# Mixing stage: the sums and differences of each chunk stored by SyncE instead of GpSimd

## The chip, the cores and the metric

The kernel runs on one core of one Trainium2 chip. The metric is device time in microseconds (us), the median over the runs.

## What is computed

The reference works on an input of 4 batches x 32 channels x 128 x 128 pixels in float32. A first layer (an attention over spectral convolutions) comes first and takes about two thirds of the time. The change lies in the second layer, which is a full spectral convolution:

```
x = x + irfft2( sum_i rfft2(norm(x))[b, i, :, :] * W[i, o, :, :] )      # W complex, 32 x 32 x 128 x 65
```

For each frequency the 32 input channels are mixed into 32 output channels by a complex matrix of its own. The weights are two float32 tensors, real and imaginary, of 34 MB each, and every one of their rows is read once.

## The kernel before

The second layer is a block of its own (the last `with ExitStack()` in the code, `p8`), and its mixing stage goes through 32 chunks (`NCHK`). A chunk `c_` holds two rows of frequencies and the two mirrored ones, and each of its buffers exists twice; `u = c_ % 2` picks one.

- **Weights.** `load_weights(eng, p, c_)` issues two transfers, real and imaginary, of 520 KB each (32 x 32 runs of 520 bytes) into the halves of `wsl[u]`. SyncE issues the pair for `p = 0`, ScalarE the pair for `p = 1`. Both wait until the chunk two before has been mixed (`s_ms`), because that frees the buffer. The last chunk takes two rows that don't lie side by side, and its pair of SyncE comes in runs of 260 bytes.
- **Columns.** GpSimd copies the columns of the spectrum of the chunk two ahead into `cols` (L1978, L1979).
- **Spectrum.** TensorE's `spectrum` (L2022) makes the spectrum rows of a chunk. ScalarE's and VectorE's `rows` copy them into `xsl[u]`, tile `pa`.
- **Mixing.** TensorE's `mix` (L2035) waits for all four weight transfers of the chunk (`s_w[u]`), for the rows, and for the PSUM tile `po[u]`. It makes 130 small matmuls and then raises `s_ms`. The trace holds two records for each of them.
- **Pairing.** ScalarE copies the lower half (`neg`, L2109). VectorE's `pairs(c_)` makes sums and differences into `osl[:, u]` (L2176 to L2187) and raises `s_oc`.
- **Storing.** GpSimd's `store(c_)` waits for the pairs and issues two transfers of 128 KB from `osl` to the DRAM tensor `os_` (L1988), in runs of 512 bytes. `pairs(c_ + 2)` waits until they have landed (`s_os[u]`).

After the 32 chunks SyncE waits for all stores and loads `os_` back in pieces (L1949). TensorE, ScalarE and VectorE turn these back into pixels, and SyncE stores the output (L1955, four transfers of 128 KB in runs of 512 bytes for each piece). The matrices for that, `eo` and `cf`, are loaded by SyncE behind the last weight load (L1941).

Each engine takes its instructions in order, and so does each engine's queue of transfers. SyncE's transfers are on queue q1 of the profile, ScalarE's on q10, GpSimd's on q0, where software makes the descriptors. All of them use the same 16 DMA engines.

Of the kernel before, what the change touches and what calls it, by code (L numbers as in the profile page):

```python
# [14 lines left out]
NB, NT, NHD = 4, 32, 32  # L15
# [22 lines left out]
SL = 2  # L38
NCHK = HH // 2 // SL
SM = SL * KWF  # L40
NP = HH // 2
# [146 lines left out]
def wait(eng, sem, value):  # L188

    if not (isinstance(value, int) and value <= 0):  # L190
        eng.wait_ge(sem, value)


def per_batch(eng, body):

    body(0)
    with eng.Fori(1, NB) as b:
        body(b)
# [8 lines left out]
def build(nc, a, c, out):  # L207
# [5 lines left out]
    def dram(name, shape):  # L213
        return nc.dram_tensor(name, shape, F32, kind="Internal").ap()
# [10 lines left out]
    os_ = dram("os_", (HH, 4, NT, NB * 32))  # L225
# [6 lines left out]
    def sems(name, n):  # L232

        return [sem(f"{name}_{i}") for i in range(n)]

    def sem(name):
        assert name not in names
        names.add(name)
        h = nc.alloc_semaphore(name=name)
        if name not in POOL_TRANSFERS:  # L240
            held.append(h)
        return h


    with top:
# [44 lines left out]
        with ExitStack() as p1:  # L290
            def sb(name, shape):
                return p1.enter_context(nc.sbuf_tensor(name, shape, F32))
# [66 lines left out]
            @block.sync  # L359
            def _(sp):  # L360
                for i in range(4):
                    n = HH * WW // 4
                    sp.dma_start(xa[:, i * n:(i + 1) * n], xf[:, i * n:(i + 1) * n]).then_inc(s_x[i // 2], 16)

                def load(b):
                    for u in range(GPB):

                        wait(sp, s_f1, GPB * b + u + 1 - GPB)
                        sp.dma_start(xd[:, u, :].rearrange("h (g w) -> h g w", g=GI),
                                     x[bass.ds((b * GPB + u) * GI, GI)].rearrange("g h w -> h g w")).then_inc(s_xd[u], 16)  # L370
                per_batch(sp, load)
                sp.wait_ge(s_mtr, 1)
                sp.dma_start(mpl.rearrange("m (z k h) -> k (m z) h", z=2, k=KW), mtr.rearrange("w m r h -> w (m r) h")).then_inc(s_wv, 16)

                def spectra_back(b):
                    for q in s_xs:
                        sp.wait_ge(q, 16 * (GPB // 2) * (b + 1))
                    sp.dma_start(room[32 * b:32 * b + 32, 0:2 * M2], xs[32 * b:32 * b + 32].rearrange("i m k -> i (m k)")).then_inc(s_xt, 16)
                for b in range(1, NB - 1):
                    spectra_back(b)  # L380
                sp.wait_ge(s_wt, 1)
                spectra_back(0)
                spectra_back(NB - 1)
                sp.wait_ge(s_wv, 16)
# [982 lines left out]
        def lagged(b, u, k, body, *args):  # L1367

            if k > u:
                if not (isinstance(b, int) and b == 0):  # L1370
                    body(b - 1, u - k + GPB, *args)
            else:
                body(b, u - k, *args)
# [497 lines left out]
        with ExitStack() as p8:  # L1871
# [20 lines left out]
            osl = sb("osl", [128, 2, 2, SL, NB, 32])  # L1892
# [14 lines left out]
            s_ms, s_nc, s_oc, s_pt8 = sem("chunk_mixed"), sem("lower_mixed_copied"), sem("mixed_chunk_paired"), sem("p8_pair_steps")  # L1907
            s_os = sems("mixed_chunk_stored", 2)
# [6 lines left out]
            def load_weights(eng, p, c_):  # L1915

                u = c_ % 2
                if p == 1:
                    row0, step = HH // 2 - SL * (c_ + 1), 1
                elif c_ < NCHK - 1:  # L1920
                    row0, step = HH // 2 + 1 + SL * c_, 1
                else:
                    row0, step = HH // 2, HH // 2 - 1
                for r, w in enumerate((a["L1_conv_weight_real"], a["L1_conv_weight_imag"])):
                    q = slice(64 * p + 32 * r, 64 * p + 32 * r + 32)
                    if step == 1:
                        src, dst = bass.AP(w.tensor, row0 * KWF, [[NT * HH * KWF, NT], [HH * KWF, NT], [1, SM]]), wsl[u][q]
                    else:
                        src = bass.AP(w.tensor, row0 * KWF, [[NT * HH * KWF, NT], [HH * KWF, NT], [step * KWF, SL], [1, KWF]])
                        dst = wsl[u][q].rearrange("p o (q w) -> p o q w", q=SL)  # L1930
                    eng.dma_start(dst, src).then_inc(s_w[u], 16)  # L1931

            @block.sync
            def _(sp):
                for t, n in ((gmean, "gmean"), (wide, "wide")):
                    sp.dma_start(t[:, :], c[n]).then_inc(s_ld, 16)
                for c_ in range(NCHK):
                    wait(sp, s_ms, c_ - 1)
                    load_weights(sp, 0, c_)
                for t, n in ((eo, "eo"), (cf, "cf")):  # L1940
                    sp.dma_start(t[:, :], c[n]).then_inc(s_eo, 16)  # L1941

                for q in s_os:
                    sp.wait_ge(q, 32 * NCHK // 2)

                def load(b, u):
                    g = GPB * b + u
                    wait(sp, s_h, g + 1 - GPB)
                    sp.dma_start(od[:, u], os_[:, :, bass.ds(2 * g, 2), :].rearrange("s f o m -> s f (o m)")).then_inc(s_od[u], 16)  # L1949

                def store(b, u):
                    g = GPB * b + u
                    sp.wait_ge(s_fin, g + 1)
                    for i in range(NB):
                        sp.dma_start(xob[:, i, bass.ds(2 * g, 2), :], yb[:, i, bass.ds(2 * g, 2), :]).then_inc(s_st, 16)  # L1955

                def body(b):
                    for u in range(GPB):
                        lagged(b, u, 0, load)
                        lagged(b, u, 3, store)  # L1960
                per_batch(sp, body)
                for k in (3, 2, 1):
                    store(NB - 1, GPB - k)
                sp.wait_ge(s_st, 16 * NB * NGRP)

            @block.gpsimd
            def _(pool):
                y1v = y1[:, :, :].rearrange("w i (s k) -> w k s i", s=2)

                def columns(c_):  # L1970

                    u = c_ % 2
                    wait(pool, s_sp, c_ - 1)
                    if c_ < NCHK:
                        near = y1v[:, SL * c_ + 1:SL * c_ + 3]
                        if c_ == NCHK - 1:
                            pool.wait_ge(s_b0, 1)
                        nc.gpsimd.tensor_copy(cols[:, u, 0:2], near if c_ < NCHK - 1 else y1v[:, 0:64:63])  # L1978
                        nc.gpsimd.tensor_copy(cols[:, u, 2:4], near).then_inc(s_col, 1)  # L1979
                    else:  # L1980
                        nc.gpsimd.memset(cols[:, u, 0, 0, 0:1], 0.0).then_inc(s_col, 1)

                def store(c_):
                    u = c_ % 2
                    pool.wait_ge(s_oc, c_ + 3)
                    n = NT * 4 * NB * 32
                    for e in range(2):
                        pool.dma_start(bass.AP(os_.tensor, (NP * e + SL * c_) * n, [[NB * 32, 128], [n, SL], [1, NB * 32]]),  # L1988
                                       osl[:, u, e].rearrange("p q b m -> p q (b m)")).then_inc(s_os[u], 16)
                columns(0)  # L1990
                columns(1)
                for v in range(2):
                    pool.wait_ge(s_col, 2)
                    wait(pool, s_zero, v)
                    nc.gpsimd.memset(xsl[v], 0.0).then_inc(s_zero, 1)
                pool.wait_ge(s_zero, 2)
                for c_ in range(NCHK):
                    columns(c_ + 2)
                    store(c_)
                for q in s_os:  # L2000
                    pool.wait_ge(q, 32 * NCHK // 2)

            @block.tensor
            def _(pe):
# [227 lines left out]
```

## Time and profile before

| | |
|---|---|
| median of 3 runs | 1069.66 us (1069.3 to 1073.97) |
| the profiled execution | 1070.72 us, of which the span of instructions 1069.1 us |
| the mixing stage | from 676 us (first weight load) to 991 us (last store landed) |
| TensorE busy over the span | 75% |
| mean DMA rate over the span | 177 GB/s |

The trace gives for each engine the instructions with their start and length. A chain of waits leads back from the last instruction to what released each step. For the queues it gives packets, bytes, and the time that the packets took as a share of the time of 16 DMA engines. These shares can add up to more than 100%, because packets of one DMA engine overlap. A line of the chain that names a tensor after "DMA" is the landing of that transfer.

### The profile page before, as it was taken

The page shows a single profiled execution, that of the slowest core. Times are in us where ns is not written, and L with a number is a line of the kernel's source. Part 1 is how long each engine was busy: PE and PEld are TensorE (multiplying, and loading weights), DVE is VectorE, ACT ScalarE, POOL GpSimd, SP SyncE. Part 2 cuts the span into 40 slices and gives each one's busy share as a digit, 9 for nine tenths or more (in the row PEclk, how much of TensorE's full clock was granted, in tenths as well). Part 3 has the DMA queues.
Part 4 walks back from the last instruction along what each step waited for, and adds up shares of the span by engine and source line. Part 5 has one row for each costly group of instructions (what it writes and reads, how often), then busy time and mean ns, then how long its engine had stood idle before and what let it go on. Part 6 is the DMA issues. An engine that isn't in the chain of part 4 may idle for free. (4 is left out here: it accounts for less than half of the span.)

```text
span 1069.1 us, 36892 instructions
## 1 busy us (share of the span) xinstructions
PE 799.1 (75%) x16113; PEld 589.4 (55%) x16113; DVE 678.4 (63%) x1459; ACT 403.4 (38%) x915; POOL 368.1 (34%) x262
## 2 busy tenths in 40 slices
PE   0499296989999846999905999366677777777797
PEld 0365142322222216888705999366666667666686
DVE  4897388778888784566568999635544444553132
ACT  0298252122323263555533666323333333331121
POOL 0022373889999801111100000324434444442000
PEclk9999598899999967999957999788888888988899
DMA  9566633465555230454122665769999999997687
GB/s 364 112 188 160 137 73 104 148 255 190 182 176 183 97 79 22 155 129 114 42 67 79 175 182 158 161 153 272 262 262 266 265 266 266 269 268 164 182 243 216
DMA packets 270336, 189.43 MB, mean 177 GB/s; under 512 B 29396, under 2 KB 259509, under 8 KB 269045
## 3 DMA queue, kind: packets, MB, share of 16 engines
q1 hardware_dynamic: 190003, 131.56, 45.9%
q10 hardware_dynamic: 75138, 44.14, 17.1%
q0 software_dynamic: 5120, 12.75, 4.2%
q8 instruction: 45, 0.74, 0.3%
q14 instruction: 30, 0.25, 0.1%
HBM read 154.50 MB, written 33.07 MB: 175 GB/s over the span
## 5 line engine op out<-in xcount | busy, mean ns | idle before, releaser
L2035 PE MATMUL po<-pa,room 128*32 128x16 f32 x8320 | 148.0, 220 | 85.7 <-DMA room<-_L_conv_weight_imag_dram 59.0
L2035 PEld LDWEIGHTS po<-pa,room 128*32 128x32 f32 x8320 | 145.2, 163 | 94.0 <-issue 78.9
L981 POOL TENSOR_TENSOR q<-lead 128x1536 f32<-128x1536 f32 (+1 forms) x51 | 170.2, 3365 | 28.0 <-POOLq L650 13.8
L1080 DVE TENSOR_TENSOR q<-pw,lead 128x1536 f32<-128x1536 f32 (+1 forms) x85 | 140.6, 1704 | 15.7 <-PE acc L1026 10.2
L2176 DVE TENSOR_TENSOR osl<-po,neg 128x128 f32<-128x128 f32 x64 | 18.4, 287 | 151.2 <-ACT neg L2109 151.2
L1026 PE MATMUL acc<-q,pt 128*32 128x384 f32 (+1 forms) x1088 | 102.4, 486 | 14.3 <-DVE q L1080 14.3
L1988 POOL DMA_DIRECT2D os_<-osl x64 | 45.3, 713 | 184.0 <-DVE osl L2187 176.1
L1978 POOL COPY cols<-y 128x512 f32<-128x512 f32 x32 | 38.3, 1197 | 145.2 <-POOLq L1744 139.8
L2109 ACT ACTIVATE neg<-po 128x272 f32<-128x272 f32 x32 | 12.7, 397 | 199.7 <-issue 184.7
L2022 PE MATMUL px<-wbat,cols 128*32 128x130 f32 x2176 | 76.3, 293 | 3.0 <-DVE wbat L2147 3.0
L1026 PEld LDWEIGHTS acc<-q,pt 128*32 128x32 f32 x1088 | 27.5, 109 | 87.1 <-issue 57.2
L1381 PE MATMUL pz<-eh,ts 128*33 128x128 f32 x1024 | 64.5, 280 | 6.2 <-DMA ph<-const_ph_dram 3.8
L2022 PEld LDWEIGHTS px<-wbat,cols 128*32 128x32 f32 x2176 | 66.8, 119 | 3.7 <-DVE wbat L2147 3.1
L920 ACT ACTIVATE ms<-pm,vec 128x512 f32<-128x512 f32 x32 | 22.0, 688 | 122.0 <-PE pm L913 114.0
L1389 PE MATMUL pi<-cw,zs 97*128 97x128 f32 x512 | 64.1, 278 | 2.4 <-ACT zs L1512 1.1
L1381 PEld LDWEIGHTS pz<-eh,ts 128*33 128x33 f32 x1024 | 56.7, 141 | 14.0 <-issue 8.1
L1389 PEld LDWEIGHTS pi<-cw,zs 97*128 97x128 f32 x512 | 59.6, 192 | 5.1 <-ACT zs L1512 3.0
L2201 DVE TENSOR_TENSOR yall<-yall,po 128x1024 f32 (+1 forms) x16 | 19.5, 1221 | 57.6 <-PE po L2063 57.6
L2158 DVE COPY pa<-px 32x260 f32<-32x260 f32 x128 | 49.6, 425 | 4.6 <-PE px L2022 3.3
L885 DVE TENSOR_TENSOR room<-gt,tp 128x1408 f32<-128x1408 f32 x26 | 41.3, 1619 | 8.9 <-PE psc L832 5.2
L392 POOL DMA_DIRECT2D xs<-xst x16 | 14.3, 895 | 94.4 <-ACT xst L426 94.4
L1462 POOL DMA_DIRECT2D ys<-yo x16 | 13.2, 824 | 94.6 <-DVE yo L1577 94.6
(335 smaller groups left out, 1582.5 us busy)
## 6 DMA issues: line engine op xcount, KB each, us to landing
room<-_L_conv_weight_real_dram ACTq DMA_DIRECT2D x32, 520.0 KB, 9.8
room<-_L_conv_weight_imag_dram ACTq DMA_DIRECT2D x32, 520.0 KB, 12.6
room<-_L_conv_weight_real_dram SPq DMA_DIRECT2D x32, 520.0 KB, 7.1
room<-_L_conv_weight_imag_dram SPq DMA_DIRECT2D x32, 520.0 KB, 10.4
lead<-xns SPq DMA_DIRECT2D x64, 192.0 KB, 3.1
lead<-wv SPq DMA_DIRECT2D x16, 576.0 KB, 5.9
yall<-in_x_dram SPq DMA_DIRECT2D x4, 2048.0 KB, 14.5
xd<-in_x_dram SPq DMA_DIRECT2D x16, 512.0 KB, 4.2
```

The lines of the kernel that those rows point to most:

```text
L885: V.tensor_tensor(z[:, j % 2, :, 0:NDV], bc(bc(w, 1, NB), 3, NT), bc(xx, 2, NDV), ALU.mult).then_inc(s_z, 1)
L920: nc.scalar.activation(ms[:, u], pm[u][:, :], ACT.Identity, bias=v1("cbeta")).then_inc(s_mc, 1)
L981: nc.gpsimd.tensor_tensor(q2[:, t % 2, :, :, 0:m], bc(weights(blk, n), 2, NB), spectra(blk), ALU.mult).then_inc(s_qp, 1)
L1026: e = nc.tensor.matmul(acc[u][rows, 0:3 * m].rearrange("p (r m) -> p r m", r=3), pt[:, k, rows], qk[:, :, b, 0:m], start=(k == 0), stop=(k ...
L1080: V.tensor_tensor(q1[:, t % 2, :, :, 0:m], bc(pw[t % 4][:, 0:3 * m].rearrange("p (r m) -> p r m", r=3), 2, NB), spectra(blk), ALU.mult).th ...
L1381: m = nc.tensor.matmul(pz[64 * v:64 * v + KW, 128 * i:128 * i + 128], ts[:, u % 2, :, i], eh[:, 128 * v:128 * v + 128], start=True, stop=True)
L1389: m = nc.tensor.matmul(pi[:, 128 * i:128 * i + 128], zs[0:KP, u % 2, i, :], cw[:, :], start=True, stop=True)
L1978: nc.gpsimd.tensor_copy(cols[:, u, 0:2], near if c_ < NCHK - 1 else y1v[:, 0:64:63])
L1988: pool.dma_start(bass.AP(os_.tensor, (NP * e + SL * c_) * n, [[NB * 32, 128], [n, SL], [1, NB * 32]]), osl[:, u, e].rearrange("p q b m -> ...
L2022: m = nc.tensor.matmul(px[u][g:g + 32, o:o + 2 * KWF], cols[:, u, q if p == 0 else 3 - q, s, 32 * b:32 * b + 32], wbat[:, b, at:at + 2 * K ...
L2035: e = nc.tensor.matmul(po[u][32 * g:32 * g + 32, 512 * q + 16 * m:512 * q + 16 * m + 16], wsl[u][:, :, q * KWF + KWF - 1 - kw], xsl[u][:, ...
L2158: V.tensor_copy(re[:, b].rearrange("i q c w -> i q (c w)"), src[:, b].rearrange("i q c w -> i q (c w)"))
```

## The change

GpSimd no longer stores anything in the mixing stage. It only copies columns. SyncE issues both stores of chunk `c_ - 2` right behind the weight loads of chunk `c_`, with the same wait for the pairs, and the stores of the last two chunks behind the loop. The shapes of the transfers and the semaphores are the same. GpSimd's wait at the end for all stores goes; SyncE has had the same wait all along. The loads of `eo` and `cf` now come behind the last stores.

```diff
@@ block.sync
+                def store_pairs(c_):
+                    u = c_ % 2
+                    sp.wait_ge(s_oc, c_ + 3)
+                    n = NT * 4 * NB * 32
+                    for e in range(2):
+                        sp.dma_start(bass.AP(os_.tensor, (NP * e + SL * c_) * n, [[NB * 32, 128], [n, SL], [1, NB * 32]]),
+                                     osl[:, u, e].rearrange("p q b m -> p q (b m)")).then_inc(s_os[u], 16)
                 for c_ in range(NCHK):
                     wait(sp, s_ms, c_ - 1)
                     load_weights(sp, 0, c_)
+                    if c_ >= 2:
+                        store_pairs(c_ - 2)
+                for c_ in range(NCHK - 2, NCHK):
+                    store_pairs(c_)
                 for t, n in ((eo, "eo"), (cf, "cf")):
                     sp.dma_start(t[:, :], c[n]).then_inc(s_eo, 16)
@@ block.gpsimd
-                def store(c_):
-                    u = c_ % 2
-                    pool.wait_ge(s_oc, c_ + 3)
-                    n = NT * 4 * NB * 32
-                    for e in range(2):
-                        pool.dma_start(bass.AP(os_.tensor, (NP * e + SL * c_) * n, [[NB * 32, 128], [n, SL], [1, NB * 32]]),
-                                       osl[:, u, e].rearrange("p q b m -> p q (b m)")).then_inc(s_os[u], 16)
                 for c_ in range(NCHK):
                     columns(c_ + 2)
-                    store(c_)
-                for q in s_os:
-                    pool.wait_ge(q, 32 * NCHK // 2)
```

## Rows read from the trace of the kernel before

**Rows 1.** Chain of waits, 760 to 1008 us: start us, us, what.

```profile
763.38 4.48 PE po L2035 x247
...
804.25 0.57 ACTq L1931
...
804.86 12.77 DMA room<-_L_conv_weight_imag_dram
...
817.85 4.47 PE po L2035 x247
...
961.34 4.52 PE po L2035 x238
...
966.60 14.38 DMA room<-_L_conv_weight_imag_dram
...
987.54 0.28 issue
...
988.53 2.21 DMA os_<-osl
```

**Rows 2.** Timeline, 799 to 820 us: start us, us, engine, line, operation.

```profile
807.53 0.14 DVE L2187 TENSOR_TENSOR osl<-po,neg 32x4 f32<-32x4 f32 x1
...
807.97 1.42 POOL L1988 DMA_DIRECT2D os_<-osl  x2 [5.09 <-DVE osl L2187]
...
813.62 0.56 SPq L1931 DMA_DIRECT2D room<-_L_conv_weight_real_dram  x1
```

**Rows 3.** Queues and issues, 760 to 960 us: packets, MB, share; KB each, median us to landing.

```profile
DMA packets 94336, 53.03 MB, mean 265 GB/s; under 512 B 2124, under 2 KB 92923, under 8 KB 94331
q1 hardware_dynamic: 46261, 23.69, 54.4%
q10 hardware_dynamic: 45958, 23.53, 51.8%
q0 software_dynamic: 2112, 5.77, 8.2%
...
room<-_L_conv_weight_imag_dram SPq DMA_DIRECT2D x23, 520.0 KB, 10.4
room<-_L_conv_weight_imag_dram ACTq DMA_DIRECT2D x23, 520.0 KB, 12.5
...
os_<-osl POOLq DMA_DIRECT2D x44, 128.0 KB, 5.4
```

**Rows 4.** Queues, 685 to 692 us, both weight queues at work and no store.

```profile
DMA packets 4025, 2.08 MB, mean 297 GB/s; under 512 B 61, under 2 KB 4024, under 8 KB 4024
```

**Rows 5.** Queues, 814.2 to 815.2 us.

```profile
DMA packets 219, 0.11 MB, mean 106 GB/s; under 512 B 15, under 2 KB 219, under 8 KB 219
```

**Rows 6.** Queues, 696 to 698.5 us, before any store.

```profile
q1 hardware_dynamic: 66, 0.03, 6.3%
```

**Rows 7.** Queues, 693 to 695.5 us, SyncE's weight load alone.

```profile
DMA packets 851, 0.45 MB, mean 179 GB/s; under 512 B 7, under 2 KB 850, under 8 KB 850
```

**Rows 8.** L1988, all its instructions: ns min/median/max, first and last start us.

```profile
L1988 POOL DMA_DIRECT2D os_<-osl x64: 710/713/738, 707.8 to 988.5; - x64
```

**Rows 9.** L1955, the output stores: ns, first and last start; us to landing.

```profile
L1955 SPq DMA_DIRECT2D out_dram<-yall x64: 378/390/1042, 1004.3 to 1066.7; - x64
...
DMA to landing us min/median/max: 1.9/2.3/4.1
```

**Rows 10.** L1931, SyncE's imaginary loads from 690 us on: ns min/median/max, first and last start us.

```profile
L1931 SPq DMA_DIRECT2D room<-_L_conv_weight_imag_dram x30: 666/666/5132, 703.3 to 966.6; - x30
```

**Rows 11.** Waits of SyncE's queue, 760 to 960 us: us in total, times, longest us.

```profile
SPq L1931 <- PE po L2035: 170.0, 22, 8.1
```

**Rows 12.** Queues, 1060.3 to 1062.3 us, output stores alone.

```profile
GB/s 266 287 297 297 246 276 307 195 184 133 205 266 297 276 287 276 276 256 226 113 154 174 277 297 297 287 287 287 297 205 164 31 0 0 0 0 0 0 0 0
...
q1 hardware_dynamic: 804, 0.39, 65.8%
```

**Rows 13.** Queues, 957 to 958 us, while a store flows.

```profile
DMA packets 568, 0.33 MB, mean 325 GB/s; under 512 B 32, under 2 KB 555, under 8 KB 568
```

## The prediction

> **What bounds the kernel now.** I read four views, in this order: the chain of waits, the queues with their issues, the queues again in short windows, and the timeline of one chunk.
>
> The chain [rows 1] runs through the weight loads. A mix ends, ScalarE issues the real and the imaginary load of the chunk two ahead (804.25), the imaginary one lands 12.77 us after its issue (804.86), and TensorE mixes that chunk. Each round does two chunks. The mixes at 763.38 and 961.34 lie 11 rounds apart, so a chunk costs (961.34 - 763.38) / 22 = 9.0 us. TensorE's 4.5 us are half of that, and GpSimd's 1.42 us of issuing [rows 2] lie beside it. Whoever shortens an engine's work here gains nothing. Only the moment at which the slowest of four weight transfers lands counts.
>
> The queues [rows 3] say why that takes long: 265 GB/s through the whole stretch. A chunk moves 4 x 520 KB + 2 x 128 KB = 2.39 MB. While both weight queues work and no store is near, the rate is 297 GB/s [rows 4]; at that rate a chunk would take 8.06 us, not 9.0. The missing 0.94 us shows in a short window: from 814.2 to 815.2 us only 106 GB/s flow [rows 5]. Most DMA engines have finished the old load there and the new one, issued at 813.6 [rows 2], has not begun. Yet the load that lets the mix at 817.8 start [rows 1] has not landed. So a few of the 16 DMA engines are late, and they set the landing. They were late before the first store too: from 696 us on 66 packets in 2.5 us [rows 6] are about what one engine handles (all 16 move 851 in 2.5 us when SyncE's queue works alone [rows 7], 53 each), and the first store is issued at 707.8 [rows 8]. These late engines have old loads left when the new ones begin, so they never pause. I take their work per chunk as the bound: 9.0 / 8.06 = 1.12 times that of the bulk.
>
> **The change part by part.**
>
> *GpSimd's issues.* 64 x 713 ns [rows 8] go from an engine that the chain meets only at the very last store. Worth nothing until then.
>
> *SyncE's issues and its wait.* Two more issues per chunk, bounded by 0.39 us for a 128 KB output store [rows 9] and 0.67 us for a weight load [rows 10]: 0.8 to 1.3 us. SyncE's queue waited 170 us of 200 for a mix [rows 11], which covers them. The new wait, for the pairs, is over about 3.3 us after the mix (804.25 [rows 1] to 807.53 [rows 2]). Behind it stands the next weight load, which is due 9.0 us after the last: 1.2 us for the two loads, then idle until 3.3, then 1.3 for the stores, leaves over 4 us. There is a second possible stall: SyncE's issues block when too much is outstanding, up to 5.1 us for a weight load [rows 10]. With 512 more packets outstanding I expect some issues to stretch by a few us. That costs nothing while the queue it feeds has work; if it did delay a load, the whole 9.0 us rhythm would slip (a rival below).
>
> *The store as traffic.* This is the term that counts. Before, GpSimd's queue moved 64 packets of 4 KB per chunk (2112 packets in 44 stores are 48 for each, 16 of them tiny completion writes). It took 8.2% of 200 us in 22 chunks, or 0.75 us of all 16 engines per chunk; shares add up to 114% there [rows 3], so 0.65 us of real time. On SyncE's queue the same bytes go as 512 packets of 512 B, the form that the output stores have. Lower bound, from those stores at their own packet time: 65.8% of 2 us x 16 engines / 804 packets = 26.2 ns [rows 12]; 32 packets per engine are 0.84 us, /1.14 = 0.74 us. Next, the output stores alone in the queue run at some 245 GB/s [rows 12], 262 KB / 245 = 1.07 us. Upper bound: the store pushes weight reads out of the time when both queues work into a time when SyncE's works alone, at 179 GB/s [rows 7] and not 297: 262 KB / 179 = 1.46 us. Below, that the writes pass beside the reads for what they cost now: 0.65 us, no change; a gain below that I exclude for the traffic itself, since more and smaller packets carry the same bytes. I take 0.95 us, between the first two, since part of each store will run beside ScalarE's load and part alone. On the late engines, times 1.12: 1.06 us against 0.73 now, **+0.33 us per chunk**. The bounds are 0 and (1.46 - 0.65) x 1.12 = +0.91 us. Stores 0 to 28 have a later weight load behind them; I count 28, since the first ones meet idle queues: **+9.3 us** (0 to +25).
>
> A rule speaks to this. The Trainium skill (DMA: Bandwidth & Descriptors, Queues, rings and completion order) says that a DMA engine takes turns between queues packet by packet. By it a store of 4 KB packets gets far more than its share against 520 B packets, and one of 512 B packets only an even one; that would change who waits, not the sum.
>
> *The order.* Before, a store's data flowed some 5.4 us after its issue [rows 3], in the last phase of the loads that the next mix waits for. Now it stands behind SyncE's load in the same queue, and ahead of SyncE's next load. In the steady state each load has one store in front of it either way, so the late engines gain nothing. SyncE's loads have been landing about 2 us ahead of ScalarE's (10.4 against 12.5 [rows 3]); they lose that lead and become the ones that mixes wait for.
>
> *The last load.* The load of chunk 31 on SyncE's queue is the slow one (14.38 us [rows 1]). Store 29 moves behind it (-0.7), store 28 stands in front of it in its own queue (about +1.1), and the lead of 2 us is gone, of which a part comes back as ScalarE's half is done earlier: +0.6. Together **+1.0 us** (0 to +2).
>
> *The last store.* Pairs done at 987.54, GpSimd's second issue at 988.53, landing 2.21 later [rows 1]. SyncE should start its second issue some 0.5 us after the pairs and land in 2.3 [rows 9]: **-0.4 us**. The loads of `eo` and `cf`, 128 KB, are now issued in the shadow of that landing and overlap the first load of `os_`; 0.
>
> Sum: 9.3 + 1.0 - 0.4 = +9.9 us, on 1070.72 us of the profiled execution: 1080.6. That execution is 1.1 us above the median of the runs, so **1079.5 us**.
>
> **The rivals.**
>
> *The store fills the lull (faster).* At 815 us the queues run at a third of their rate [rows 5]. If the late engines are late because of the software-made stores, or if the bulk sets the landing more than I think, then the store's 0.73 us leave the way of the load and fall into the lull: -0.65 x 28 = -18 us, less the end, 1052 us. It decides as soon as the late engines pause between loads for longer than the store takes. For it: the lull exists, and the store now flows just ahead of the landing. Against it: the late engines exist without any store [rows 6]. The Trainium skill (DMA: Bandwidth & Descriptors, Latency and other measured facts) says that two of the 16 engines are usually slower, and offers as a best guess that the rings of software-made descriptors crowd their ports. By that rule the late engines would catch up once GpSimd stores nothing.
>
> *It is hidden anyway (same).* The small writes pass beside reads for the price of the large ones, and only the ends change: about 1070 us. For it: while the old stores flow, the total goes above 297 GB/s, with 325 GB/s from 957 to 958 us [rows 13], so writes and reads may not compete fully. Against it: one queue of 512 B writes makes only 245 GB/s by itself [rows 12].
>
> *The queue itself becomes the bound (much slower).* SyncE's queue carries 1296 KB per chunk, ScalarE's 1040 KB. If they share evenly and ScalarE's stands empty for the difference, the upper bound holds, +0.91 x 28 = +25 us, with the ends 1096 us; blocked issues that delay the next weight load would add to it. Against it: the mix's wait for both loads lets ScalarE's queue be refilled while SyncE's is still full.
>
> **How the numbers follow.** Forecast, slower by 4 to 20 us: 0.48. Same: 0.26. Faster: 0.21. Much slower: 0.05. The range reaches down towards the faster case, to 1057, and up to 1092; it leaves out about half of the faster case and the far end of the slower ones, some 2 in 10. The forecast's own range is 1074 to 1090. About 0.5%, 5.3 us, is what a measurement of this kernel can tell from no change. The lowest part of the forecast, 0.02, lies within it: faster 0.21, same 0.26 + 0.02 = 0.28, slower 0.46 + 0.05 = 0.51.
>
> **What would show it.** In the queues between 760 and 960 us: q0 gone, q1 up by 512 packets per chunk, mean rate near 256 GB/s (2.39 MB in 9.33 us). In the chain: landings on SyncE's queue in place of ScalarE's, and chunks 9.3 us apart. In the issues: SyncE's imaginary load landing in 12 us or more, ScalarE's sooner than 12.5. Wrong would be a rate above 275 GB/s with no lull (the store fills it), or SyncE's weight loads issued late after the mix (the blocked queue). The prediction fails above all if the late engines are not the bound, or if they owe their lateness to GpSimd's stores.

## The result: 1.6% faster, where 0.9% slower was forecast

The changed kernel takes 1053.5 us (1051.9 to 1055.65, 4 runs) against 1069.5 for the kernel before: ratio 0.9838, 95% interval 0.9817 to 0.9859. The profiled execution has a span of 1054.0 us, 15.1 less. The time is close to the 1052 us of the first rival, "the store fills the lull".

The chain of waits after, from 745 to 990 us (start us, us, what), the counterpart of [rows 1]:

```profile
762.34 4.55 PE po L2036 x247
...
800.04 0.57 ACTq L1931
800.65 11.23 DMA room<-_L_conv_weight_imag_dram
812.11 4.53 PE po L2036 x234
...
947.27 4.52 PE po L2036 x248
951.88 0.60 SPq L1931
952.52 13.16 DMA room<-_L_conv_weight_imag_dram
965.91 4.53 PE po L2036 x240
...
972.34 0.37 SPq L1942
972.75 1.96 DMA os_<-osl
974.79 4.36 DMA room<-os_
```

The shape is that of before: mix, issue by ScalarE, landing of ScalarE's imaginary load, mix. In some rounds the view names VectorE's pairs or ScalarE's copies as what released a mix, but the code has that mix wait for earlier ones, and in both kernels each mix of chunks 5 to 28 starts 0.23 to 0.28 us after the last completion of its weight loads. So it is the landing in every round. Only the landing comes sooner, 11.23 us after its issue where it was 12.77. The mixes at 762.34 and 947.27 are the same two that stood at 763.38 and 961.34, so 22 chunks take 184.9 us and not 198.0: 8.41 us a chunk, 0.6 less. The account of the span: -1.0 up to that first mix, -13.0 in the 22 chunks, -1.2 from there to the last mix (18.64 us for 19.87), -0.8 from the end of the last mix to the first load of `os_` (4.35 us for 5.15), and +1.0 in the back transform, which I have not pursued. Together -15.0.

The queues after, 760 to 940 us (packets, MB, share of 16 engines; KB each, median us to landing), the counterpart of [rows 3]:

```profile
DMA packets 100400, 51.11 MB, mean 284 GB/s; under 512 B 2051, under 2 KB 100394, under 8 KB 100394
q1 hardware_dynamic: 56242, 28.45, 67.7%
q10 hardware_dynamic: 44152, 22.60, 52.3%
...
room<-_L_conv_weight_imag_dram SPq DMA_DIRECT2D x21, 520.0 KB, 9.4
room<-_L_conv_weight_imag_dram ACTq DMA_DIRECT2D x21, 520.0 KB, 11.2
os_<-osl SPq DMA_DIRECT2D x44, 128.0 KB, 7.6
```

Queue q0 is gone, and q1 has taken its bytes in small packets. The same 2.39 MB a chunk flow at 284 GB/s where they flowed at 265. SyncE's load still lands 1.8 us ahead of ScalarE's. The rate lies above the 275 GB/s that the prediction had named as a sign of being wrong.

SyncE's queue after, 800 to 812 us, and its waits from 760 to 940 us (us in total, times, longest):

```profile
800.04 0.57 SPq L1931 DMA_DIRECT2D room<-_L_conv_weight_real_dram  x1
800.65 0.67 SPq L1931 DMA_DIRECT2D room<-_L_conv_weight_imag_dram  x1
803.50 0.92 SPq L1942 DMA_DIRECT2D os_<-osl  x2
808.38 0.57 SPq L1931 DMA_DIRECT2D room<-_L_conv_weight_real_dram  x1
```

```profile
SPq L1931 <- PE po L2036: 83.5, 21, 4.6
SPq L1942 <- DVE osl L2188: 47.5, 22, 2.3
```

The wait for the pairs and the stores' issue fit between two mixes, and each load is issued the moment its mix ends.

**Where in a chunk the bytes flow.** The trace has every packet. Averaged over 20 chunks, with time counted from the start of the issue of a chunk's real load, the queues move this much (GB/s in steps of 0.5 us; q1 SyncE, q10 ScalarE, q0 GpSimd):

```
us after issue  -1.0  -0.5   0.0   0.5   1.0   1.5   2.0   2.5   3.0   3.5   4.0   4.5
before  q1        67    71   104    31    17    74   210   247   128   126   145    98
before  q10       69    69   176   261   126    47    26    20    67   100   128   187
before  q0       195   215    59     2     0     0     0     0     0     0     0     0
after   q1       150   148   149   149   150   150   210   284   184   130   120   135
after   q10      143   149   153   161   166   149   102    17    26    70   116   155
```

New loads bring their first data some 1.3 us after the issue on SyncE's queue and 3 to 3.5 us after it on ScalarE's. Before, q0 pushes the old loads down to some 70 GB/s each in the last microsecond ahead of the issue, and SyncE's queue then runs nearly dry from 0.5 to 1.5 us behind it; that is the lull of [rows 5]. After, SyncE's queue carries the store between the end of its old load and the start of its new one, and never runs dry.

The same trace has 16 small completion packets for each transfer. I call the last of the 16 the straggler. For ScalarE's imaginary load, median over 24 chunks, from the start of its own issue to the end of the 14th and of the last packet, and by how much the last is behind the 14th (a median by itself, so not the difference of the two), beside the mean spacing of chunks (the mix follows about 1 us after the last packet):

```
                  spacing us   14th of 16   last of 16   last behind 14th
before               9.05        10.15        11.69          1.54
after                8.45        10.22        10.51          0.52
none                 8.49         9.71        10.37          0.74
soft_half_only       8.78        10.08        10.97          1.09
half_soft            8.65        10.51        10.72          0.33
delay8               8.96        10.78        11.92          0.68
soft_spaced          8.95        10.70        11.50          0.82
soft_late            9.42        10.59        12.25          1.67
soft_plus_hard       9.02        11.28        11.70          0.46
hard_double          8.89        10.48        10.94          0.18
```

The other kernels are those of the experiments below. In the changed kernel the 14th completion is as late after its issue as before. What moved is the straggler: 1.5 us behind before, 0.5 after. The mix waits for the last, so the landing comes 1.2 us sooner in a round of two chunks, 0.6 a chunk. In delay8 and soft_plus_hard it is the 14th that is late, and the straggler is close: a slow chunk doesn't need a straggler.

### The profile page after: what moved, and what is told of

It is laid out like the page before. It is cut to its first block and busy times, and to the rows that moved or that the text cites. A ratio compares the mean times of both kernels' runs of the same rounds, so it can differ in the third digit from the quotient of the medians.

```text
span 1054.0 us, 36890 instructions
## 1 busy us (share of the span) xinstructions
PE 804.5 (76%) x16113; PEld 593.1 (56%) x16113; DVE 678.4 (64%) x1459; ACT 403.8 (38%) x915; POOL 320.8 (30%) x198
## 5 line engine op out<-in xcount | busy, mean ns | idle before, releaser
L2099 ACT ACTIVATE pa<-px 32x260 f32<-32x260 f32 x128 | 41.2, 369 | 9.0 <-PE px L2023 8.3
## 6 DMA issues: line engine op xcount, KB each, us to landing
room<-_L_conv_weight_imag_dram ACTq DMA_DIRECT2D x32, 520.0 KB, 11.2
```

Of the source, the lines that this page charges most:

```text
L2099: act.activation(re[:, b].rearrange("i q c w -> i q (c w)"), src[:, b].rearrange("i q c w -> i q (c w)"), ACT.Copy)
```

## The experiments

All ratios are against the kernel before on the same chip. After the result I had three theories. A: a software-made store holds one DMA engine back, whatever it carries. B: the place of the store's data counts. C: the bytes and packets of the software-made store count.

**Is it GpSimd's way of storing?** To the changed kernel I added an extra store for each chunk, by GpSimd (8 or 64 KB) or, as a control, by ScalarE.

```diff
                 for c_ in range(NCHK):
                     columns(c_ + 2)
+                    pool.wait_ge(s_oc, c_ + 3)
+                    pool.dma_start(dum[c_, 0:16, 0:128], gmean[0:16, 0:128]).then_inc(s_dum, 16)   # soft64k: 0:128
# hard64k: the same 64 KB by ScalarE behind rows(c_ + 2)
```

> The changed kernel, plus one extra store of 8 KB (16 rows of 512 B from a constant to a spare DRAM tensor) by GpSimd for each chunk, at the moment when GpSimd stored before; nearly no traffic. Theory A (a software-made store keeps one DMA engine late, whatever it carries): the last of the 16 completions of a weight load comes 1 us or more behind the others again, chunks 8.7 to 9.0 us apart, 1062 to 1070 us. Theory B (the place of the store's data in time: behind SyncE's load it fills the lull, before it stood in front of the landing): 1053 to 1055 us. Theory C (the bytes and packets of a software-made store): 1053 to 1056 us.

> The changed kernel, plus one extra store of 64 KB (128 rows of 512 B) by GpSimd for each chunk. Theory A: as with 8 KB, plus 64 KB / 297 GB/s = 0.22 us a chunk, 1066 to 1074 us. Theory B: only the extra bytes just ahead of the landing, at most 0.22 x 28 = 6 us, 1056 to 1060 us. Theory C: between no change and the bytes' share, 1056 to 1062 us.

> Control for the 64 KB case: the changed kernel, plus the same extra 64 KB by ScalarE on its own hardware queue, behind the copies of each chunk. Theory A: no late engine, 1053 to 1058 us, well below the software-made one. Theories B and C: as the software-made one within 2 us.

Measured: 8 KB by GpSimd 1054.2 us, ratio 0.9848 (0.9825 to 0.9871), as the changed kernel. 64 KB by GpSimd 1057.2 us, 0.9866 (0.984 to 0.9892). 64 KB by ScalarE 1057.3 us, 0.9886 (0.9856 to 0.9917). Theory A falls: the software path by itself costs nothing that shows at 8 KB, and at 64 KB it costs what ScalarE's hardware path costs, within the intervals.

**Is it the place, with GpSimd still storing?** Three kernels keep GpSimd's stores, with columns copied one chunk earlier so that nothing waits for them, and move the stores in time.

```diff
                 for c_ in range(NCHK):
-                    columns(c_ + 2)
-                    store(c_)
+                    if c_ + 3 < NCHK + 2:
+                        columns(c_ + 3)
+                    # delay8: wait for the pairs, eight memsets of `wide`; soft_spaced: these between the two halves
+                    # soft_late: pool.wait_ge(s_ms, min(c_ + 2, NCHK))
+                    store(c_)
```

> The kernel before, with GpSimd's columns copied one chunk earlier and a pause of some 3.5 us on GpSimd (eight clearings of a matrix that is no longer needed) ahead of each pair of stores, so that the stores' data flows behind the landing of the weight load and not ahead of it. Software-made stores still. Theory A: the late engine stays, 1062 to 1070 us. Theory B: the gain of the change is had with GpSimd's stores too, 1052 to 1058 us. Theory C: 1064 to 1070 us.

> The kernel before, with columns one chunk earlier and a pause of some 3.5 us on GpSimd between the two stores of a chunk: the same software-made bytes as two bursts of 128 KB. If a burst of 256 KB ahead of the landing is what costs, most of the gain: 1055 to 1061 us. If the path costs, 1064 to 1070 us.

> The kernel before, GpSimd storing everything, with columns copied one chunk earlier and each store held back until the next chunk has been mixed, so that its data should flow some 5 us after the following weight loads are issued, behind the landing that the next mix waits for. If the place of the data sets the time, the gain of the change is had by GpSimd too: 1053 to 1058 us, the last completion of a weight load within 0.5 us of the others. If software-made stores of this size hold one DMA engine back wherever they flow: 1064 us or more, last completion 1 us or more behind.

Measured: delay8 1070.4 us, 0.9981 (0.9956 to 1.0006). soft_spaced 1071.5 us, 0.9981 (0.9955 to 1.0006). soft_late 1081.8 us, 1.0102 (1.0071 to 1.0132). None came near the times that I had expected if the place alone counted. The pause was 3.0 us, not 3.5. In the trace, q0 flowed from 0.5 to 4 us after the issue in delay8, in two parts (until just behind the issue, and 1 to 3.5 us) in soft_spaced, and from 3.5 to 7 us in soft_late. None of these places is free: in delay8 q1, with SyncE's new load, moved 15, 75 and 148 GB/s from 1.5 to 3 us, where before had 74, 210 and 247. So "behind the landing" was too coarse. None of them put the store exactly between SyncE's old and new load, and whether GpSimd could gain there was not tried.

**Which hardware queue?**

```diff
 # by_act: both stores by ScalarE behind rows(c_ + 2); split: e = 0 by SyncE, e = 1 by ScalarE
+                    act.wait_ge(s_oc, c_ + 3)
+                    for e in range(2):
+                        act.dma_start(bass.AP(os_.tensor, ...), osl[:, c_ % 2, e]...).then_inc(s_os[c_ % 2], 16)
```

> The changed kernel with all stores issued by ScalarE on its hardware queue, behind the copies of each chunk, none by SyncE or GpSimd. Theory A (software-made stores keep a DMA engine late): any hardware queue gives the gain, 1051 to 1057 us. Theory B (the place behind SyncE's load is what counts): ScalarE's load is the one that mixes wait for, and a store in front of the next one delays it, 1060 us or more.

> The changed kernel with the first half of each store (sums) by SyncE and the second (differences) by ScalarE, both on hardware queues. Both theories: 1050 to 1055 us; if the two queues are then filled more evenly, a few us below the changed kernel.

Measured: by_act 1065.5 us, 0.992 (0.9901 to 0.9939). split 1056.4 us, 0.9839 (0.9823 to 0.9856), as the changed kernel. Both are hardware queues with the same packets, so it counts which of them has the store. by_act still gains 8 us on the kernel before, so that much doesn't need SyncE's queue. On ScalarE's queue the store stands behind the load that lands last and ahead of the next one that will land last. On SyncE's it has 1.8 us of lead to stand in. ScalarE's imaginary loads also took longer to issue in by_act, 2.04 us (median) where the changed kernel has 0.94, and by_act doesn't separate this from the place.

**What does the store still cost, and how much of it was GpSimd's?** `none` leaves out all stores of the stage, `soft_half_only` has only the differences, by GpSimd, and `half_soft` has sums by SyncE and differences by GpSimd.

```diff
 # none
-                    if c_ >= 2:
-                        store_pairs(c_ - 2)
-                    wait(dve, s_os[u], 32 * (c_ // 2))
-                    sp.dma_start(od[:, u], os_[...]
+                    sp.dma_start(od[:, u], xf[:, 0:1024]...
 # soft_half_only: before, with `for e in (1,)` in GpSimd's store, and the last line too
 # half_soft: `for e in range(1)` in store_pairs, and the e = 1 transfer by GpSimd behind columns(c_ + 2)
```

> The changed kernel without any store in the mixing stage; the inverse transform reads rows of the input in place of the stored pairs (stores and their waits are left out, the later work has the same size). It gives the floor. If the store lies wholly in the lull: the same as the changed kernel less the last store, 1049 to 1053 us. If its bytes still cost their time at 297 GB/s: 0.88 x 28 = 25 us less, about 1028 us.

> The changed kernel with sums stored by SyncE and differences by GpSimd, each 128 KB a chunk. Theory A: the late engine is back in full, 1062 to 1070 us. Theory B or C: half of the gain, about 1061 us; so the late completion in the trace decides, 1.5 us behind under A, less than 0.8 under C.

> The kernel before with GpSimd storing only the differences (128 KB a chunk, one transfer); the sums are not stored, and the inverse transform reads rows of the input in place of the stored pairs, the same size. If the amount stored by software is what holds one DMA engine back: last completion within 0.5 us of the others, 1053 to 1058 us. If a hardware store on SyncE's queue is what lets that engine catch up, and here is none: last completion 1 us or more behind, 1060 to 1068 us.

Measured: none 1054.5 us, 0.9825 (0.9808 to 0.9841); soft_half_only 1063.3 us, 0.9914 (0.9882 to 0.9947); half_soft 1059.5 us, 0.9866 (0.9848 to 0.9883).

The queues without any store, 760 to 940 us:

```profile
DMA packets 88647, 45.43 MB, mean 252 GB/s; under 512 B 1373, under 2 KB 88641, under 8 KB 88641
...
room<-_L_conv_weight_imag_dram SPq DMA_DIRECT2D x22, 520.0 KB, 9.7
room<-_L_conv_weight_imag_dram ACTq DMA_DIRECT2D x22, 520.0 KB, 11.3
```

This is the clearest single run. Without stores the queues move 252 GB/s, well below the 284 of the changed kernel, and a chunk still takes 8.5 us. The imaginary load lands 11.3 us after its issue against 11.2 with SyncE's stores. The stage is bound by the round of issue, first data, landing and mix, in which the weights' own bytes take their part, and the changed kernel's store costs nothing in it that shows (0.9825 and 0.9838, intervals overlap). And half_soft, with one store more than soft_half_only, is no slower: its profiled chunks are 8.65 us apart against 8.78, its straggler 0.3 us behind against 1.1. The closest test of the path is half_soft beside split, which differ only in who stores the differences, GpSimd (1059.5 us) or ScalarE (1056.4): at 128 KB GpSimd's is some 3 us slower, and the intervals just overlap.

**Twice the bytes.** `soft_plus_hard` is the kernel before plus 256 KB of extra stores by SyncE behind its loads; `hard_double` is the changed kernel plus the same.

```diff
                     load_weights(sp, 0, c_)
+                    sp.wait_ge(s_oc, c_ + 1)
+                    for e in range(2):
+                        sp.dma_start(bass.AP(dum.tensor, (2 * c_ + e) * 2 * 128 * 128, [[128, 128], [128 * 128, 2], [1, 128]]),
+                                     wide[:, 0:256].rearrange("p (q m) -> p q m", q=2)).then_inc(s_dum, 16)
```

> The kernel before, GpSimd storing everything, plus 256 KB of extra stores by SyncE behind each pair of its weight loads (in the form of the changed kernel's stores, from a constant to a spare DRAM tensor). Twice the stored bytes. If the hardware store on SyncE's queue lets the late engine catch up: last completion within 0.6 us of the others, and about the time of before, 1065 to 1075 us, in spite of the bytes. If software-made stores of this size hold it back: 1 us or more behind, and 0.88 us a chunk for the bytes, 1085 to 1095 us.

> Control for the last one: the changed kernel plus the same 256 KB of extra stores by SyncE behind its own, all on the hardware queue, the same bytes in all. The last completion within 0.5 us of the others. The bytes exceed what the lull holds, so 0.3 to 0.9 us a chunk: 1062 to 1078 us. Its distance to the other is what the software-made half costs at equal bytes.

Measured: soft_plus_hard 1070.3 us, 0.9964 (0.9947 to 0.9982). hard_double 1070.8 us, 0.9985 (0.9962 to 1.0008). Their queues, 760 to 940 us, soft_plus_hard first:

```profile
DMA packets 95737, 53.02 MB, mean 295 GB/s; under 512 B 2558, under 2 KB 94449, under 8 KB 95729
q1 hardware_dynamic: 52223, 26.41, 60.6%
q10 hardware_dynamic: 41586, 21.29, 49.0%
q0 software_dynamic: 1920, 5.25, 8.3%
```

```profile
DMA packets 106360, 53.83 MB, mean 299 GB/s; under 512 B 2625, under 2 KB 106354, under 8 KB 106354
```

The kernel before can carry 256 KB more per chunk without getting slower, if SyncE's queue carries them behind its load; the straggler comes down to 0.5 us. Beside none (0.9825), the four cases are: 256 KB on SyncE's queue, 0.9838; 256 KB by GpSimd, 1; both, 0.9964; 512 KB on SyncE's queue, 0.9985. The first 256 KB on SyncE's queue are free, with or without GpSimd's. GpSimd's 256 KB cost 0.0175 alone (19 us) and 0.0126 beside SyncE's (13 us). A second 256 KB on SyncE's queue cost 0.0147 (16 us).

The two kernels with 512 KB take about the same time, but not for the same reason, so they don't say that it makes no difference how descriptors are made. In hard_double SyncE's own issues are held up. This is SyncE's queue there, one chunk from 811 to 820 us:

```profile
811.49 0.57 SPq L1933 DMA_DIRECT2D room<-_L_conv_weight_real_dram  x1
812.10 2.86 SPq L1933 DMA_DIRECT2D room<-_L_conv_weight_imag_dram  x1
815.00 2.74 SPq L1944 DMA_DIRECT2D os_<-osl  x2
817.78 2.50 SPq L1954 DMA_DIRECT2D dum<-wide  x2
```

Issuing fills 8.5 of the 8.9 us of a chunk, where it takes 2.1 in the changed kernel and 3.3 in soft_plus_hard. The next weight load is issued up to 1.0 us after its mix, and SyncE's imaginary load now lands 11.6 us after its issue against ScalarE's 11.0. This is the blocked queue that the prediction had as its last rival; it takes twice the stores to bring it about.

**Two more moves of work on SyncE's queue.** `hard_mid` puts the stores between SyncE's real and imaginary load. `share8` lets SyncE load a quarter of ScalarE's imaginary part, to make both queues land together.

```diff
 # hard_mid, in load_weights
                     eng.dma_start(dst, src).then_inc(s_w[u], 16)
+                    if between and r == 0:
+                        between()                      # store_pairs(c_ - 2)
 # share8: ScalarE loads dst[:, 8:] of its imaginary part, SyncE the rest behind its own two
+                    eng.dma_start(wsl[u][q][:, 0:8], src).then_inc(s_w[u], 16)
```

> The changed kernel with SyncE issuing its real load, then the stores of two chunks before, then its imaginary load: hardware stores, but ahead of half of the load that the mix waits for, while both queues are busy. If the place sets the time: 0.88 us a chunk back, 1066 to 1075 us. If software-made stores are what costs: 1053 to 1058 us.

> The changed kernel with a quarter of ScalarE's imaginary load (8 of 32 output channels, 130 KB) issued by SyncE, behind its own two loads and ahead of the stores. ScalarE's load lands some 1.8 us after SyncE's in the changed kernel. If the landing of the later queue sets the rhythm, both now land together, 0.9 us earlier than ScalarE's did, half of which comes off each chunk: 1053.5 - 0.4 x 28 = 1042 us. If the start of the load sets it, no change.

Measured: hard_mid 1121.0 us, 1.0442 (1.0398 to 1.0487); share8 1067.2 us, 0.9946 (0.9919 to 0.9973). In hard_mid SyncE's imaginary load had to wait for the pairs, and the chain shows what came of it:

```profile
803.74 0.49 SPq L1944
804.27 12.16 DMA room<-_L_conv_weight_imag_dram
816.42 0.23 issue
816.65 4.47 PE po L2036 x244
```

SyncE's imaginary load is issued at 804.27, 3.8 us later than ScalarE's (800.48), and lands 12.2 us after that, though the queues move only 220 GB/s; the load was issued late and landed late, with queues that were less full than in any other kernel here. It is no test of the place, since two things changed. In share8 SyncE's issues are held up too (1.8 us for its imaginary load where the changed kernel has 0.67, 2.1 for the extra piece). The extra piece is issued 1.8 us after ScalarE's real load in a typical round (807.23 for 805.41) and takes 10.2 us from there (median), and the chain of waits runs through it. What I had moved off ScalarE's queue became the last landing on SyncE's, and the gain is lost. Neither version beats the changed kernel, nor does any other here.

## Why the prediction was wrong

- **The bound (failed, and the rest with it).** "These late engines have old loads left when the new ones begin, so they never pause. I take their work per chunk as the bound." If that were so, no kernel could move much more than the 265 GB/s of before at these bytes; the changed kernel moves 284 and hard_double 299. And without stores a chunk takes 8.5 us at 252 GB/s. The bound is a round trip: mix 4.5 us, then 11.2 us or more from issue to landing, two chunks per round. A store in a pause of that round was free, one that pushed the landing was not.
- **The evidence for it.** The observation of [rows 6] was right: one engine was late before any store, and it is 2.1 us late at that point in the changed kernel too. But I took a single event for a state. In the changed kernel the straggler of ScalarE's imaginary load lies behind by, chunk after chunk,

```
chunks 4 to 21: 0.3 1.6 1.1 0.9 0.5 0.3 0.3 0.1 0.1 0.1 1.0 0.7 0.5 0.4 0.2 0.1 1.3 0.9
```

  and fades after each jump. The jumps at chunks 14 and 20 follow instruction packets of 8 KB (q14) at 815 and 867 us; that these cause them is the order in time only, not a test, and a packet of the same kind at 759 us is followed by no jump. In the kernel before it stays between 1.1 and 1.9 us in all chunks from 5 to 30. In the kernel before, too, it had faded to 0.4 and 0.2 us at chunks 3 and 4 (725 and 734 us) before it came back to 1.2 at chunk 5; these completions would have raised the question.
- **The order of the data (failed).** "In the steady state each load has one store in front of it either way, so the late engines gain nothing." Counting stores per load was right, and missed that SyncE's queue had a gap of its own between loads, some 0.5 to 1.5 us after each issue.
- **The cost of the traffic (failed, in size and sign).** +0.33 us a chunk was expected; -0.6 was measured. The prediction gave the store 1.06 us on SyncE's queue against 0.73 on GpSimd's, and excluded a gain for the traffic itself: its lower bound was that the store still costs what it did. On SyncE's queue it costs nothing that shows (none against after). What it had cost on GpSimd's was sized well: 0.0175 of 1073 us is 19 us, 0.67 a chunk over 28, close to the 0.65 that the rival gave it.
- **SyncE's lead (failed).** It was not lost: SyncE's imaginary load lands after 9.4 us, ScalarE's after 11.2, and the chain stays with ScalarE's.
- **The last load (failed).** +1.0 expected, -1.2 measured: it landed after 13.16 us and not 14.38. I take the reason to be that of all other chunks; no run tests it by itself.
- **The last store (right way, half the size).** -0.4 expected, -0.8 measured up to the first load of `os_`.
- **SyncE's issues (right).** The wait for the pairs (47.5 us in 180) and the issues cost nothing. The stretched issues that I feared did not show in the steady stage of this kernel (the longest took 0.9 us); weight loads are issued at the end of each mix. They did show with twice the stores, in hard_double.
- **The rivals.** "The store fills the lull" gave -0.65 a chunk and 1052 us, and had a chance of 0.21. What I had against it, the straggler without a store, was the misread evidence. Its number came true, and the part that is shown is that a store on SyncE's queue costs nothing; that it runs in the lull is what the trace shows. It named a second cause, that software-made stores make the engines late. The Trainium skill (DMA: Bandwidth & Descriptors, Latency and other measured facts) has this as its best guess for two slow engines. The runs speak against it as the only cause: 8 and 64 KB by GpSimd leave the straggler as small as it is (0.4 and 0.3 us behind), with all of GpSimd's stores and SyncE's beside them it is 0.5 us behind, and without any store it still jumps to 2.1 us at times. The Trainium skill's rule of turns by packet (DMA: Bandwidth & Descriptors, Queues, rings and completion order) agrees with the trace in direction: 4 KB packets of q0 take up to 241 GB/s where the two load queues get 57 and 58. By even turns it would be some 8 times as much as each of them, an estimate from the packet sizes and that rule; measured are 4 times.

**What stays open.** What makes GpSimd's 256 KB cost 19 us. The store differs from SyncE's in three things at once: it is made by software, it goes as packets of 4 KB, and it flows at another time and beside the loads, not behind one. So theory C stands open beside theory B. No kernel changes one of the three alone at 256 KB, and whether a store by GpSimd would be free in exactly SyncE's gap was not tried. Also open is why the straggler lingers. It is 0.2 to 0.5 us behind in the four kernels of the table with a store behind SyncE's load, 0.7 without any store, and 0.7 to 1.7 with GpSimd's alone. The runs show this pairing, and not what happens inside that engine.

## What to carry to other kernels

Before calling a stage bound by bandwidth, take the bytes away: here 252 GB/s without stores and 284 GB/s with SyncE's gave the same chunks of 8.5 us, and 265 GB/s gave 9.0; it was a round trip with pauses. Then look at each queue by its phase in the round: a transfer queued behind the load that lands early, ahead of that queue's next one, was free at 256 KB; the same bytes by GpSimd, or a second time on that queue, cost 13 to 19 us. Look also at how long the queue's issues take: with too much outstanding the issuing engine itself is held up (2.7 us for one issue in hard_double, 0.67 in the changed kernel). An odd engine seen once is an event; follow it over ten rounds, and in a kernel without the suspect, before making it the bound.

## What the runs showed of the hardware

- One hardware queue alone moved 179 GB/s of 520-byte reads ([rows 7]), two 297 ([rows 4]), and with writes of 512 bytes beside them the mean rose to 299 (hard_double).
- With both load queues empty or nearly so and both issues at the same moment (chunks 2 and 3 of before, after and none), the first data came 1.35 us after the issue on SyncE's queue and 2.6 to 2.8 us after it on ScalarE's. In the steady stage it is 1.3 and 3 to 3.5 us, about the 1.8 us that ScalarE's load lands later. At the start of the stage ScalarE issued 0.8 us ahead of SyncE, and there its data came after 1.5 us and SyncE's after 4.8 to 5.2. So it is not ScalarE's queue as such that is slow; there the one that issued first was served first.
- Issues on a hardware queue were held up with much outstanding: 2.7 us (median) for SyncE's imaginary load in hard_double, 0.67 in the changed kernel.
- GpSimd's stores of 512-byte rows went as packets of 4 KB, 32 for each 128 KB, and held two thirds of the DMA rate while they flowed (241 of 356 GB/s); its 8 KB store went as 16 packets of 512 bytes.
